# A decoder layer with a mixture of experts on one core: closing steps spread over two, the mixture begun a step earlier, three quarters of the output rows normalised during the last expert tiles

## What is computed

```python
q, k, v = split(x @ Wq.T + bq), split(x @ Wk.T + bk), split(x @ Wv.T + bv)   # 16 heads of 16
q, k = softmax(q, axis=-1), softmax(k, axis=-2)        # k: over the 1024 tokens of a batch
state = einsum('bhnd,bhne->bhde', k, v)
out = layernorm(einsum('bhnd,bhde->bhne', q, state)) * ln_g + ln_b
x = layernorm(x + out @ Wo.T + bo)
x = layernorm(x + cross_attention(ctx, x, mask))       # 8 heads on 77 context keys
w, idx = top_k(softmax(x @ router_w), 4)               # 4 of 8 experts
x = layernorm(x + sum_over_4(w * (gelu(x @ up_w[e]) @ down_w[e])))      # 256 -> 1024 -> 256
```

## Time and profile before

| | us |
|---|---|
| median of 3 runs | 1259.43 (1258.27 to 1266.05) |
| span of the profiled execution | 1256.1 |
| PE busy | 1096.2 (87%) |
| DVE busy | 764.7 (61%) |
| POOL busy | 645.5 (51%) |
| ACT busy | 495.2 (39%) |

### The profile page before, as it was taken

How to read it: one execution, slowest core, us unless ns; L and a number is a source line. 1 busy time by engine, 2 the same in 40 slices (tenths; PEclk the granted TensorE clock), 3 DMA queues, 4 the chain that set the end, 5 groups by cost and what they waited for, 6 DMA issues and landing times.

```text
span 1256.1 us, 27061 instructions
## 1 busy us (share of the span) xinstructions
PE 1096.2 (87%) x8572; PEld 904.3 (72%) x8572; DVE 764.7 (61%) x1863; ACT 495.2 (39%) x913; POOL 645.5 (51%) x736
## 2 busy tenths in 40 slices
PE   6568977878887699988899999999999999999960
PEld 3345665656655488877788888888888888888750
DVE  2667978987897687754844444444444444444326
ACT  3754534544343255553233333333333333333214
POOL 3012317756673777766775455555555555554324
PEclk9878979979896799998999999999999999999985
DMA  6421223222212333433444654555544445563326
GB/s 176 154 91 59 93 75 104 74 65 80 77 38 64 72 62 76 71 64 68 65 76 77 134 85 77 77 77 77 77 77 77 77 77 77 77 77 60 64 55 243
DMA packets 163039, 105.07 MB, mean 84 GB/s; under 512 B 107596, under 2 KB 153856, under 8 KB 162656
## 3 DMA queue, kind: packets, MB, share of 16 engines
q1 hardware_dynamic: 132896, 67.67, 21.4%
q0 software_dynamic: 30016, 35.68, 19.7%
HBM read 51.91 MB, written 36.04 MB: 70 GB/s over the span
## 4 chain that ended last, share of the span: by engine, by line
PE 65%; DVE 15%; POOL 9%; issue 5%; DMA 3%; ACT 3%; SPq 0%; POOLq 0%; ACTq 0%; DVEq 0%
PE big L1663 25%; PE big L1682 13%; PE trans L1682 11%; PE big L1705 3%; POOL slot_records L779 3%; PE big L1604 2%; PE small L1751 2%; PE small L1615 2%; POOL early_sums L809 2%; PE trans L1533 2%; POOL rstd L755 1%; PE small L1583 1%; PE big L1707 1%; DVE stat L1047 1%; DVE w_down L1043 1%
## 5 line engine op out<-in xcount | busy, mean ns | idle before, releaser
L1663 PE MATMUL big<-xgT,w_up 128*128 128x256 f16 (+1 forms) x3456 | 408.0, 267 | 12.7 <-DMA xgT<-xg 10.1
L1663 PEld LDWEIGHTS big<-xgT,w_up 128*128 x3456 | 324.7, 98 | 55.9 <-issue 16.4
L902 ACT ACTIVATE h<-big,up_scale 128x512 f32<-128x512 f32 x270 | 185.5, 687 | 451.4 <-PE big L1663 437.6
L1296 DVE TENSOR_SCALAR hh<-h,h_scale 128x512 f16<-128x512 f32 x270 | 133.8, 496 | 312.5 <-ACT h L902 310.8
L809 POOL DMA_INDIRECT token_sums<-y,rec x99 | 163.2, 1649 | 244.5 <-ACT y L910 223.5
L1682 PE MATMUL big<-w_down,hh 128*128 x1264 | 216.8, 274 | 2.8 <-DVE hl L1298 2.5
L1298 DVE SCALAR_TENSOR_TENSOR hl<-h,h_scale,hh 128x512 f16<-128x512 f32 x270 | 203.0, 752 | 9.6
L1682 PE MATMUL big<-w_down,hl 128*128 x632 | 173.0, 274 | 0.0
L1682 PE MATMUL trans<-w_down,hh 128*128 x896 | 152.8, 273 | 2.6 <-DVE hl L1298 2.4
L779 POOL DMA_INDIRECT slot_records<-recs,posi x128 | 130.2, 1017 | 35.3 <-issue 33.6
L1682 PEld LDWEIGHTS big<-w_down,hh 128*128 128x128 f16 x1264 | 123.2, 98 | 20.8 <-issue 3.8
(11 more groups left out here) (249 smaller groups left out, 1512.4 us busy)
## 6 DMA issues: line engine op xcount, KB each, us to landing
w_down<-in_L_ffn_up_w_dram SPq DMA_DIRECT2D x8, 1024.0 KB, 5.0
w_down<-in_L_ffn_down_w_dram SPq DMA_DIRECT2D x7, 1024.0 KB, 5.7
XA<-in_x_dram SPq DMA_DIRECT2D x32, 128.0 KB, 2.6
XRES<-in_x_dram SPq DMA_DIRECT2D x32, 128.0 KB, 2.4
token_rows<-XR SPq DMA_DIRECT2D x32, 128.0 KB, 1.8
sums<-token_sums SPq DMA_DIRECT2D x8, 512.0 KB, 7.2
out_dram<-sums SPq DMA_DIRECT2D x8, 512.0 KB, 2.6
xgT<-xg SPq DMA_TRANSPOSE x135
```

The costliest lines, as they stand in the source:

```text
L902: act.activation(h[:, i % H_RING, :], psu[up_bank(i)], ACT.Gelu_apprx_tanh, scale=k["up_scale"][:, t:t + 1]).then_inc(gelu_ready, 1)
L1296: dve.tensor_scalar(hh[:, i % HALF_RING, :], h[:, i % H_RING, :], k["h_scale"][:, t:t + 1], None, ALU.mult).then_inc(hh_ready, 1)
L1663: ins = pe.matmul(psu[up_bank(i)][:, j * size(t):(j + 1) * size(t)], w[:, ws, c, m:m + P], xgT[:, t % 2, xs * CC + c, 0:size(t)], start=(n ...
```

## The change

1. Closing work is spread. A step before the closing step is now `ending(s)` (s = 7, 16, 25, 34): turning of key maxima, their reduction, the spreading and `shift_keys` stand there. In the closing step ACT's exponentials stand ahead of the context work, PE's state products right behind the context logits, and `build_state` ahead of the value stage.
2. The layer norm of the heads' output is folded: Wo's columns are centred once (step 1), PE turns the raw Z, and `first_sum` multiplies the projection by rstd. 32 norms on DVE go.
3. PIECE_STEPS changes, MIX0 is 37 (38 before), so 12 mixed steps. The last piece has a staging place of its own in the room of wqkv and the input tiles, and waits for the last qkv product instead of the state. `early_slots` runs in step 32 instead of 36. The mask products of the context logits come ahead of the products that need x1.
4. Late expert tiles: first the full tiles whose slots lie in the first three batches (tiles 18 to 54), then the nine small ones (55 to 63), then eight full ones (64 to 71). The tables take 43 operations to the slots and 6 for the scales instead of 30 and 6, with matrices of 45 x 17.
5. After the scatter-adds of tile 63, SP loads the 24 rows per partition of the first three batches (six loads of 512 KB, issued at tile 66). DVE takes their sums and moments in groups 246 to 263, POOL the deviations of four rows behind the scatter-adds of tiles 66 to 70, ACT normalises all 24 rows behind the gelus of groups 253 to 269 and further. Behind the last tile 8 rows are left: four loads of 256 KB, DVE and ACT normalise two of four each. Of the stores of ahead rows five stand ahead of the last wait for y and one behind the last loads.

```diff
-ETILES = FULL + BLOCKS - SB * FULL
+SINGLES = BLOCKS - SB * FULL
+ETILES = FULL + SINGLES
+AHEAD = B - 1
+SINGLE0 = (TOPK * N * AHEAD + EXP * (SLOTS - 1)) // SLOTS
+LAST0 = SINGLE0 + SINGLES
...
-PIECE_STEPS = [2, 3, 4, 5, 6, 7, 8, 9, 12, 15, 18, 21, 24, 28, 32, 36]
+PIECE_STEPS = [2, 3, 4, 5, 7, 9, 11, 12, 13, 16, 18, 21, 23, 27, 30, 35]
...
+def ending(s):
+
+    return closing(s + 1)
...
-    return SB if t < FULL else 1
+    return 1 if SINGLE0 <= t < LAST0 else SB
...
-            return V[:, :, :, :].rearrange("p t c m -> p (t c m)")[:, 0:CC * HID]
+            return load_place[:, :]
...
+        STAT0 = NGROUPS - 24
+        STAT_GROUPS = 18
...
+        def rows_at(i):
...
+            q = i - STAT0
+            if 0 <= q < STAT_GROUPS:
+                return range(q * AHEAD_ROWS // STAT_GROUPS, (q + 1) * AHEAD_ROWS // STAT_GROUPS)
...
+        def rows_known(g):
+
+            return next(i for i in range(STAT0, NGROUPS) if rows_at(i).stop >= (g + 1) * G)
...
+        def norms_at(i):
+
+            return [g * G + i - rows_known(g) - 5 for g in range(AHEAD_GROUPS) if 0 <= i - rows_known(g) - 5 < G]
...
-                    sp.wait_ge(sm_ready, SM["st", B - 1, CC - 1] + 1)
+                    sp.wait_ge(big_ready, BIG["qkv", NT - 1] + 1)
...
+                if t == LAST0 + 2:
+                    sp.wait_ge(table_step, SCALE_STEPS)
+                    for u in (LAST0 - 2, LAST0 - 1):
+                        sp.wait_ge(y_added[u % 2], moved(u))
+                    for g in range(AHEAD_GROUPS):
+                        sp.dma_start(sums[:, g * G:(g + 1) * G, :], ahead_in[:, g * G:(g + 1) * G, :]).then_inc(sums_loaded[g], 16)
+
+            def store_ahead(g):
+                sp.wait_ge(normed_s, (g + 1) * G)
+                sp.dma_start(ahead_out[:, g * G:(g + 1) * G, :], sums[:, g * G:(g + 1) * G, :]).then_inc(stored, 16)
+
+            for g in range(AHEAD_GROUPS - 1):
+                store_ahead(g)
             for t in (ETILES - 2, ETILES - 1):
                 sp.wait_ge(y_added[t % 2], moved(t))
...
-            for g in range(GROUPS):
-                sp.wait_ge(normed_v, (g + 1) * BY_DVE)
...
+            for i in range(len(last_loaded)):
+                at = slice(AHEAD_ROWS + i * PART, AHEAD_ROWS + (i + 1) * PART)
+                sp.dma_start(sums[:, at, :], last_in[:, i * PART:(i + 1) * PART, :]).then_inc(last_loaded[i], 16)
+            store_ahead(AHEAD_GROUPS - 1)
...
+            def deviations(g):
+                at = slice(g * G, (g + 1) * G)
+                pool.wait_ge(fmv_ready, (g + 1) * G)
...
+                for g in range(AHEAD_GROUPS):
+                    if t == GROUP[rows_known(g)][0] + 1:
+                        deviations(g)
...
+                b = closing(s)
+                if b is not None:
+                    for q in range(KG):
+                        act.wait_ge(ks_ready, KG * b + q + 1)
+                        at = slice(q * TB // KG, (q + 1) * TB // KG)
+                        act.activation(K[:, at, :], K[:, at, :], ACT.Exp).then_inc(ke_ready, 1)
...
             for i in range(MIXED_GROUPS, NGROUPS):
                 gelu(i)
                 t, _ = GROUP[i - LAG]
                 if i - LAG == last_group(t):
                     results(t)
+                for r in norms_at(i):
+                    normed_row(r)
             results(ETILES - 1)
-
-            for g in range(GROUPS):
-                act.wait_ge(fshift_ready, g + 1)
-                for i in range(g * G + BY_DVE, (g + 1) * G):
-                    act.activation(sums[:, i, :], sums[:, i, :], ACT.Identity, scale=frstd[:, i:i + 1], bias=fshift[:, i:i + 1]).then_inc(normed_s, 1)
+            for i in range(NGROUPS, NGROUPS + G + 5):
+                for r in norms_at(i):
+                    normed_row(r)
+            for g in range(AHEAD_GROUPS, GROUPS):
+                for r in range(g * G + BY_DVE, (g + 1) * G):
+                    normed_row(r)
...
+                tabled(dve.tensor_tensor(cmpn, ahead_counts[:, :].unsqueeze(2).to_broadcast([P, EXP, PER // 2]),
+                                         steps[:, 0:PER:2].unsqueeze(1).to_broadcast([P, EXP, PER // 2]), ALU.is_gt))
+                tabled(dve.tensor_reduce(blocks[:, :], cmpt, AX_X, ALU.add))
+                tabled(dve.tensor_reduce(pairs[:, :], cmpt[:, :, 1:PER:2], AX_X, ALU.add))
+                tabled(dve.tensor_reduce(near[:, :], cmpn, AX_X, ALU.add))
+                tabled(dve.tensor_tensor(near[:, :], near[:, :], pairs[:, :], ALU.min))
+                tabled(dve.tensor_tensor(length[:, 0:EXP], near[:, :], taken[:, :], ALU.subtract))
+                tabled(dve.tensor_tensor(length[:, EXP:SEGS], pairs[:, :], near[:, :], ALU.subtract))
...
+                tabled(dve.tensor_tensor(got[:, :], length[:, 0:EXP], length[:, EXP:SEGS], ALU.add))
...
                 tabled(dve.tensor_tensor_scan(endb[:, :], ones[:, 0:EXP], blocks[:, :], 0.0, ALU.mult, ALU.add))
...
+                tabled(dve.tensor_tensor(past[:, :, 1:SEGS + 1], iof[:, 0:PAIRS].unsqueeze(2).to_broadcast([P, PAIRS, SEGS]),
+                                         ends[:, :].unsqueeze(1).to_broadcast([P, PAIRS, SEGS]), ALU.is_ge))
+                tabled(dve.tensor_tensor(hots[:, :, :], past[:, :, 0:SEGS], past[:, :, 1:SEGS + 1], ALU.subtract))
...
+                dve.wait_ge(rstd_ready[0], g + 1)
                 if g >= 3:
                     dve.wait_ge(r2_ready, g - 2)
-                dve.tensor_tensor(X1[:, g % 3, :], y_[:, 0:C], XRES[:, g % 2, :], ALU.add).then_inc(sm_free, 1)
+                dve.scalar_tensor_tensor(out=X1[:, g % 3, :], in0=y_[:, 0:C], scalar=rstd[:, 0, g % 4:g % 4 + 1], in1=XRES[:, g % 2, :],
+                                         op0=ALU.mult, op1=ALU.add).then_inc(sm_free, 1)
...
+                    dve.wait_ge(sm_free, SM["wo", c1] + 1)
+                    sums_of(1, c1, X1[:, c1 % 3, :])
...
+                if end is not None:
+                    key_maximum(end)
...
-                if c0 is not None:
-                    norm(0, c0, Z[:, :], z_ready)
-                if c2 is not None:
-                    logit_shift(c2)
...
                     norm(1, c1, X1[:, c1 % 3, :], x1_ready)
                 if c2 is not None:
+                    logit_shift(c2)
                     shifted_logits(c2)
+                if close is not None:
+                    if piece is not None:
+                        split_low(piece)
+                    build_state(close)
...
+                if end is not None:
+                    shift_keys(end)
...
+                if s == COUNT_STEP + 1:
                     dve.wait_ge(sm_free, SM[("early",)] + 1)
                     early_slots()
...
+                for r in rows_at(i):
+                    row_sums(r)
+                for r in rows_at(i):
+                    row_moments(r)
+
+            for r in range(AHEAD_ROWS, NT + 1):
+                if r < NT:
+                    row_sums(r)
+                if r > AHEAD_ROWS:
+                    row_moments(r - 1)
+                if r == NT - 2:
+                    norm_group(AHEAD_GROUPS)
...
+                    pe.wait_ge(mask_ready, g // TB + 1)
+                logits = big_into(("lg", g))
+                halves_ = [logits[:, LOGIT0 + c * XPC * KEYS:LOGIT0 + (c + 1) * XPC * KEYS] for c in range(CC)]
+                for dst in halves_:
+                    pe.matmul(dst, one16[:, :], mbf[:, :, :].rearrange("p h k -> p (h k)"), start=True, stop=False)
...
+                for c, dst in enumerate(halves_):
+                    ins = pe.matmul(dst, x1T[:, c, :], kbd[:, c, :, :].rearrange("p h k -> p (h k)"), start=False, stop=True)
...
                 if c1 is not None:
-                    pe.wait_ge(z_ready, c1 + 1)
+                    pe.wait_ge(sm_free, SM["out", c1] + 1)
                     turn("z", c1, Z[:, :])
...
+                if end is not None:
+                    pe.wait_ge(kmx_ready, TB * (end + 1))
+                    dst = small_into(("km", end))
...
                 if close is not None:
...
+                if c3 is not None:
+                    context_values(c3)
+                if c4 is not None:
+                    turn_second(c4)
+                    route(c4)
+                if end is not None:
+                    pe.wait_ge(kdiag_ready, CC * (end + 1))
+                    pe.matmul(small_into(("kb", end))[:, 0:C], ones[:, :], kdiag[:, :, :].rearrange("p c t -> p (c t)"),
+                              start=True, stop=True).then_inc(sm_ready, 1)
```

312 lines of the change are left out of this document (169 added, 143 removed).

## The result

| | median us | executions | span of the profiled one |
|---|---|---|---|
| before | 1260.07 (1257.76 to 1271.11) | 20 | 1256.1 |
| after | 1253.28 (1244.24 to 1258.01) | 20 | 1256.3 |

The ratio of after to before is 0.9923, 95% interval 0.9905 to 0.9941. 1216 was forecast, 1203 to 1235 the range. The time is outside it, the direction is right.

A forecast was written before the change was run, and what follows sets the result against it. PE was taken to bound plain steps, mixed steps and late tiles, and a four-engine chain the closings. Terms summed to -43.5 us, taking the span from 1256.1 to 1212.6; with 3.3 the median was 1216, range 1203 to 1235.

The forecast's parts named there:

- The tail: Behind the last matmul: 24.1 us after the change against 41.45 before, -17.3 us.
- the holds of ScalarE: Last expert tiles: ScalarE's early row norms wait for POOL and delay gelus at groups 256, 259 and 268, +7 us.
- the start of the mixture: From step 35 to the first expert product: 32 us instead of 51.1, -19.1 us.
- the burst of loads: Six row loads at tile 66, ahead of tile 67's transposes: costed at nothing, up to +10 us without cover.
- I give 3.5 of the 6.1 back: Batch 3's plain steps: 3.5 us saved of the 6.1 us they take over eight steps of 9.65 us.
- 4.5 back: Batch 4 to step 34: plain steps save 4.5 us of the 9.1 us over eight steps of 9.65 us.
- The prediction's own sign of being wrong: Forecast wrong if plain steps exceed 10.4 us, PE waits for xgT at tile 67, or ending steps outgrow the closing's saving.
- my one rival on the clock: Last eight tiles: ScalarE's holds idle PE and they run at 1.2 GHz, +84 us, 1300 us; chance 0.02.
- A piece leaves: Batch 3: one weight piece moves out of it, part of the reason for 3.5 us saved in plain steps.
- Pair after: 11.5 + 9.65 + 3.3 = 24.5: Closing step plus the step ahead of it: 24.5 us against 32.6 before, -8 us a pair.
- My rival on DVE: Front: DVE bounds it, so only 10 of 28.8 us come, 1235 us; chance 0.11.
- The twelfth mixed step costs 16.3 less 1.5: The added mixed step costs 16.3 us less 1.5 for one missing chain tile, +14.8 us.

The follow-up runs named there:

- the five profiles with this front: Profiles of the kernel after, its unedited repeat and three edited versions with the same front code (one up to step 36); first expert products start at 402.5 to 413.8 us.
- best kernel: Kernel after with ScalarE's row norms three groups later, step 37's transposes ahead of the context loads, and shares turned ahead of the projection: 0.9704, 1225.4 us.
- after_again: The kernel after run once more with no edit, against the kernel before: ratio 0.9952.

## Why the forecast was wrong

**Right.** The tail (24.1 forecast, 25.3 measured), the holds of ScalarE with their places and their sum (+7, +7.5; next gelus late by 3.9 at group 256 and 6.4 at 259 where 3.6 and 6.2 were forecast), the start of the mixture from step 34 on (-15.8, -15.6), the tables and the tile less (-4.4, -4.8), the burst of loads (hidden: whatever it did to the transposes of tile 67, no gelu came later), the start-up (-5, -6.9), the ending step (11.9 us for step 25 of after against 9.35 of a plain one).

**The failed step, first part: the plain steps of batches 3 and 4.** "I give 3.5 of the 6.1 back" and "4.5 back" took 8 us off them; they grew by 20.8, which is 28.8 of the 42 us that the front lacks. The prediction's own sign of being wrong is there: plain steps beyond 10.4 us, 12.1 on average in both batches. My sum put the granted clock outside the closings at no change, because the earlier trace rows show 0.94 and 0.96 for these batches, and my one rival on the clock looked at the last tiles, where nothing happened. Steps 18, 19, 22, 23, 27, 28 and 32 of after are at 0.74 to 0.86 where the profile of before has 1.00. If each of the fourteen steps took the shortest time that it has in the five profiles with this front, they would take 152.4 us and not 169.0: my estimate of the clock's part is thus 17 of the 28.8 us in this profile, and less against the median. The other 12 us stay open: even these shortest times add up to 4 us more than the 148.2 of before. "A piece leaves" was misread too: both lists have three splits in batch 3, and the new one only moves the third from step 25 to step 24.

"TensorE: Matmul & The Clock Gate" of the Trainium skill (section "Part 1: The HAM clock gate") says that activity releases the throttle and idling brings it back, and that how many products a kernel runs slowly at its start differs from run to run. This case's trace agrees on the two levels and shows such a difference in mid-kernel: 9.68 and 12.35 us for one step of the same code.

**The failed step, second part: the closing.** "Pair after: 11.5 + 9.65 + 3.3 = 24.5" adds PE's work. DVE was busy 25.20 us in the pair before, of which the fold removes under 1. A pair of 24.5 asks DVE to be busy without a gap, through a chain in which PE, ACT and POOL make it wait. Measured are 26.7 and 31.1 us (the second with a weight piece). The step ahead of the closing came out at 11.9 (12.95 forecast), the closing step took 14.8 instead of 11.5, its state products 4.1 instead of 3.8. Of the 8 us for a closing, undoing the spread shows some 3 us in all, not clear of zero (after), and 8 in all (best kernel), and with the old list a pair won 0.7 and 1.4. That the pair 25+26 came near the forecast is luck: the piece list, and not the spread, took most of it.

The same holds for batch 3: I forecast 94.8 us where DVE was busy 92.27 of 106.3 and 88.45 after. My rival on DVE had the right mechanism for the closings and a chance of 0.11, but it still gave the front 10 us, where the profiles show 13.6 lost. A check that would have warned is one division per stretch, the busy time of the second busiest engine by the forecast length: 24.0 / 24.5 = 0.98 for the pair, where 0.90 came out, and 88.45 / 94.8 = 0.93 for batch 3. It is no hard limit, as DVE reaches 10.43 / 11.12 = 0.94 in step 14 of after_again.

**The first mixed step.** "The twelfth mixed step costs 16.3 less 1.5" counted PE's work. It took 22.66 since SyncE had twelve context loads ahead of the transposes. I had listed the queues of step 35 and not those of step 37: moving the start of the mixture also moves every wait of the steps that become mixed.

**A misreading without effect.** The rival on the clock puts the wait of 2.38 us at 622.65 "inside a stretch at 0.97". That stretch ends at 602.00; from 602 to 639 the clock of before is 1.00.

**Open.** What lowers the clock in one splitting step and not in another, and the 12 us of the plain steps beyond it.

## What to carry to other kernels

A change that shortens a chain over several engines is bounded by each engine's own busy time in the stretch: divide that busy time by the forecast length, engine by engine, before believing the sum. Before crediting an edit with the gain of a stretch, list everything else that moved in or out of it, here one weight piece. Where TensorE waits 1 to 2 us every few us, price the stretch at both clocks, and look for real work that can stand in the wait. When a stage begins earlier, list each queue, the issuing engine's too, for the steps that change their kind. Work put on an engine ahead of its due time should stand so late that its input is certainly there: three groups later cost nothing and gave 7 us.

## What the hardware showed that I had not expected

One kernel took 1244.2 to 1258.0 us in 20 executions, and the granted clock is the one recorded figure that goes with it (0.946 to 0.927). Ten products of about 0.26 us in each splitting step raised the clock and won 8 us in one kernel, and cost 15 us in its predecessor, where steps 20, 21 and 32 fell from 1.00 to 0.86, 0.82 and 0.85. And a fully clocked closing pair (1.00 against 0.93, with twelve added products in its waits) was not shorter, 26.6 and 26.7 us.
